# Softmax sums kept with channels on rows: a 0/1 product spreads each head's sum over its rows, VectorE divides there, and the projection follows without transposes

## What is computed

```
# self-attention
q, k, v = heads(x @ Wq + bq), heads(x @ Wk + bk), heads(x @ Wv + bv)
attn = softmax(rope(q) @ rope(k).T / sqrt(8))
out  = (attn @ v, heads side by side) @ Wp + bp
# the layer
x = x + self_attention(layernorm(x))
x = x + cross_attention(layernorm(x), ctx)     # the same form, Wo, bo
x = x + layernorm(xn + top2_experts(xn)) * gamma + beta,  xn = layernorm(x)
```

## Time and profile before

| | |
|---|---|
| median of three runs | 718.91 us (718.05 to 723.16) |
| profiled execution, its time | 726.41 us |
| profiled execution, its span | 724.6 us |
| PE busy | 586.8 us (81%) |
| DVE busy | 396.8 us (55%) |
| ACT busy | 334.2 us (46%) |
| POOL busy | 336.6 us (46%) |
| mean granted PE clock | 0.869 |
| chain that ended last: PE, DVE | 54%, 19% of the span |

### The profile page before, as it was taken

One profiled execution on the slowest core, in us unless ns is written; L12 is line 12 of the kernel. 1 busy time (PEld: TensorE's weight loads), 2 busy tenths in 40 slices (PEclk: granted clock), 3 DMA queues, 4 the chain that ended last, 5 costly groups with the idle time before them and its releaser, 6 DMA issues.

```text
span 724.6 us, 22167 instructions
## 1 busy us (share of the span) xinstructions
PE 586.8 (81%) x7694; PEld 425.6 (59%) x7695; DVE 396.8 (55%) x1325; ACT 334.2 (46%) x867; POOL 336.6 (46%) x464
## 2 busy tenths in 40 slices
PE   4638898999998898889899979841698888888791
PEld 2325665666755656656567656621597888888630
DVE  3457675767685675474563634225354444445364
ACT  2215565665755655555454633311354544445333
POOL 4415452524437446345254265355754344444365
PEclk9859999999999999898895965555799999999996
DMA  4340413140773305103112210002222211121182
GB/s 120 112 115 16 129 54 96 49 141 22 209 211 104 96 18 140 59 24 86 33 48 65 65 52 16 31 19 70 58 67 53 58 52 50 51 61 50 57 240 75
DMA packets 74424, 55.62 MB, mean 77 GB/s; under 512 B 9024, under 2 KB 70981, under 8 KB 74338
## 3 DMA queue, kind: packets, MB, share of 16 engines
q1 hardware_dynamic: 69954, 45.92, 22.5%
q0 software_dynamic: 4384, 8.53, 3.7%
HBM read 33.62 MB, written 19.23 MB: 73 GB/s over the span
## 4 chain that ended last, share of the span: by engine, by line
PE 54%; DVE 19%; issue 9%; POOL 6%; DVEq 4%; another core or an unknown queue 3%; ACT 3%; DMA 2%; SPq 1%; POOLq 0%
DVE nmp L1149 7%; PE AV L738 7%; PE AV L927 6%; PE S L915 6%; PE ST L711 5%; PE AV L831 4%; PE W L782 4%; PE SM L763 3%; DVEq L1374 3%; PE ST L717 3%; PE SM L751 2%; POOL routed L1524 2%; PE S L679 2%; DVE va L1396 2%
## 5 line engine op out<-in xcount | busy, mean ns | idle before, releaser
L1149 DVE TENSOR_REDUCE nmp<-S 128x4 bf16<-128x512 f32 (+1 forms) x256 | 142.3, 577 | 103.3 <-PE S L679 67.0
L963 ACT ACTIVATE prob<-ST 128x512 f32<-128x512 f32 (+1 forms) x256 | 138.5, 591 | 91.0 <-PE ST L717 78.8
L1083 ACT ACTIVATE va<-S,b1s 128x128 f32<-128x128 f32 x288 | 82.2, 368 | 99.3 <-PE S L915 93.1
L1586 POOL DMA_INDIRECT expert_out<-va,prob x72 | 70.9, 985 | 92.6 <-DVE va L1401 75.9
L711 PE MATMUL ST<-nmt,onesr 32*77 32x128 bf16 (+1 forms) x1024 | 82.4, 235 | 16.1 <-DVE nmp L1149 12.3
L915 PE MATMUL S<-va 128*128 128x128 f32 x576 | 81.4, 285 | 17.1 <-DVE va L1389 15.7
L738 PE MATMUL AV<-prob,va 77*32 77x128 f32 (+1 forms) x2048 | 93.9, 306 | 0.3 <-issue 0.2
L711 PEld LDWEIGHTS ST<-nmt,onesr 32*77 32x77 bf16 (+1 forms) x1024 | 59.1, 112 | 52.5 <-issue 48.5
L915 PEld LDWEIGHTS S<-va 128*128 128x128 f32 x576 | 71.3, 195 | 25.5 <-DVE va L1389 24.0
L1489 POOL TENSOR_SCALAR ve<-mv 128x1 f32<-128x1 f32 x64 | 14.8, 232 | 150.2 <-DVE mv L1183 149.9
L1524 POOL DMA_INDIRECT routed<-pay,dest x64 | 65.3, 1021 | 22.3 <-issue 16.3
(11 more groups left out here) (187 smaller groups left out, 1189.5 us busy)
## 6 DMA issues: line engine op xcount, KB each, us to landing
prob<-routed SPq DMA_DIRECT2D x72, 65.0 KB
qs<-q_parts SPq DMA_DIRECT2D x32, 128.0 KB, 3.0
ks<-k_parts SPq DMA_DIRECT2D x32, 128.0 KB
q2s<-q_parts SPq DMA_DIRECT2D x32, 128.0 KB
va<-expert_out SPq DMA_DIRECT2D x16, 256.0 KB, 4.2
k2s<-k_parts SPq DMA_DIRECT2D x32, 77.0 KB
xin<-x SPq DMA_DIRECT2D x8, 256.0 KB, 3.2
q_parts<-rpart SPq DMA_DIRECT2D x8, 256.0 KB
```

What stands on the lines that cost most here:

```text
L963: act.activation(prob[0:st.keys, j, :], ST[j % 2][0:st.keys, :], ACT.Exp, scale=SCALE).then_inc(s_exp, 1)
L1083: last = act.activation(ht[:, k, q, :], S[k][:, q * P:(q + 1) * P], ACT.Gelu, bias=b1s[:, bass.ds(b + q, 1)])
L1149: V.tensor_reduce(nmp[:, st.at % 2, row_tile(p), 0:NB], S[p % 2][:, 0:NB * st.keys].rearrange("p (b k) -> p b k", b=NB), AX.X, ALU.max, ne ...
L1586: pool.indirect_dma_start(out=expert_out, out_offset=bass.IndirectOffsetOnAxis(ap=xr[:, c % ROUND, D + 1:D + 2].bitcast(U32), axis=0), in_ ...
```

## The change

The sums stay with channels on rows. A 128 x 128 matrix of zeros and ones, `of_head`, has in row k a one in the 16 columns of a head if row k holds that head's sum. PE multiplies it with both halves of `ots` into `DEN`, so each of the 16 rows of a head gets the head's sum. DVE takes the reciprocal of the whole 128 x 256 tile and multiplies `ots` by it. The result is what the projection takes: with the weights' rows spread to the same places (`wp`, two halves), two products add up to the output, and no turn back is needed. In the padded weights the row of the first head's sum holds the bias: the sum divided by itself is 1. `wp` is made once at the start by products with a spread identity (`padded`, `first_sum`). The three-part bf16 bias (`c3`, `three_ones`) goes. `x1` has 13 rows instead of 14.

```diff
-RING = 14
+RING = 13
...
-        wself = sb("wself", [P, 2, D])
-        wcross = sb("wcross", [P, 2, D])
+        wself = sb("wself", [P, 1, D])
+        wcross = sb("wcross", [P, 1, D])
+
+        wp = sb("wp", [P, 2, 2, D])
+        of_head = sb("of_head", [P, P])
...
-        rden = sb("rden", [P, H])
-        onorm = sb("onorm", [P, H, HD])
-        onormt = sb("onormt", [P, L])
+        rden = sb("rden", [P, 2 * L])
+        onormt = sb("onormt", [P, 2 * L])
...
-        PROJ, TURNED, ROWS = SM[:, 0:D], SM[:, 0:2 * L], SM[:, 0:L]
+        PROJ, DEN = SM[:, 0:D], SM[:, 0:2 * L]
...
-            (idb[:, :], ident_bf), (wraw2, w_cross[:, 0:2, :]), (wcross[:, :, :], w_cross[:, 2:4, :]),
+            (idb[:, :], ident_bf), (wraw2, w_cross[:, 0:2, :]), (wcross[:, 0, :], w_cross[:, 2, :]), (wpraw[:, 0, :], w_self[:, 5, :]), (wpraw[:, 1, :], w_cross[:, 3, :]),
...
-            def sums_turned(st):
+            def sums(st):
+
                 pe.wait_ge(s_ot, st.at + 1)
                 if st.at:
                     pe.wait_ge(s_res, st.at)
                 for m in range(2):
-                    last = tr(TURNED[:, m * L:(m + 1) * L], ots[:, m * L:(m + 1) * L], idf[:, :])
-                last.then_inc(s_turned, 1)
-
-            def rows_turned(st):
+                    last = mm(DEN[:, m * L:(m + 1) * L], of_head[:, :], ots[:, m * L:(m + 1) * L], start=True, stop=True)
+                last.then_inc(s_den, 1)
+
+            def projected(st):
                 pe.wait_ge(s_onorm, st.at + 1)
-                tr(ROWS, onorm[:, :, :].rearrange("p h c -> p (h c)"), idf[:, :]).then_inc(s_rows, 1)
-
-            def projected(st):
-                pe.wait_ge(s_onormt, st.at + 1)
-                w = wcross[:, 1, :] if st.cross else wself[:, 1, :]
-                if st.at == 0:
-                    pe.wait_ge(s_cb, C3)
-                mm(PROJ, onormt[:, :], w, start=True, stop=False)
-                mm(PROJ, three_ones[0:96, :], c3[0:96, int(st.cross), :], start=False, stop=True).then_inc(s_proj, 1)
+                for m in range(2):
+                    last = mm(PROJ, onormt[:, m * L:(m + 1) * L], wp[:, int(st.cross), m, :], start=(m == 0), stop=(m == 1))
+                last.then_inc(s_proj, 1)
...
             pe.wait_ge(s_cb, 2)
+            pe.wait_ge(s_pad, PADS)
+            for cross in range(2):
+                for m in range(2):
+                    at = (2 * cross + m) * D
+                    last = mm(ST[1][:, at:at + D], padded[:, m, :], wpraw[:, cross, :], start=True, stop=(m == 1))
+                    if m == 0:
+                        mm(ST[1][:, at:at + D], first_sum, cfull[:, cross, :], start=False, stop=True)
+            last.then_inc(s_padded, 1)
...
                 act.wait_ge(s_av, 2 * st.at + 2)
                 if st.at:
-                    act.wait_ge(s_turned, st.at)
+                    act.wait_ge(s_onorm, st.at)
                 move(ots[:, :], SUMS, s_ot)
-
-            def rows_out(st):
-                act.wait_ge(s_rows, st.at + 1)
-                if st.at:
-                    act.wait_ge(s_proj, st.at)
-                move(onormt[:, :], ROWS, s_onormt)
...
+            act.wait_ge(s_padded, 1)
+            move(wp[:, :, :, :].rearrange("p c m d -> p (c m d)"), ST[1][:, :], s_wp)
...
-                did(V.tensor_copy(c3[:, :, :], cfull))
-                for rows in (slice(32, 64), slice(64, 96)):
-                    for quarter in range(rows.start // 32, 3):
-                        part = slice(32 * quarter, 32 * quarter + 32)
-                        did(V.tensor_tensor(cfull[part], cfull[part], c3[part, :, :], ALU.subtract))
-                        did(V.tensor_copy(c3[part, :, :], cfull[part]))
-                assert n == C3
+
+            def spread_out():
+
+                V.memset(padded, 0.0).then_inc(s_pad, 1)
+                V.memset(first_sum, 0.0).then_inc(s_pad, 1)
+                V.tensor_copy(of_head[:, :].rearrange("p (h c) -> p h c", c=VG),
+                              idf[:, HD::VG].unsqueeze(2).to_broadcast([P, P // VG, VG])).then_inc(s_pad, 1)
+                dve.wait_ge(s_pad, 3)
+                V.tensor_copy(padded.rearrange("p m (h c) -> p (m h) c", c=VG)[:, :, 0:HD],
+                              idf[:, :].rearrange("p (h c) -> p h c", c=HD)).then_inc(s_pad, 1)
+                V.tensor_copy(first_sum[:, HD:HD + 1], idf[:, HD:HD + 1]).then_inc(s_pad, 1)
...
             def norm_rows(st):
 
-                dve.wait_ge(s_turned, st.at + 1)
-                if st.at:
-                    dve.wait_ge(s_rows, st.at)
-                o = TURNED.rearrange("p (h c) -> p h c", c=VG)
-                V.reciprocal(rden[:, :], o[:, :, HD:HD + 1].rearrange("p h c -> p (h c)")).then_inc(s_rden, 1)
+                dve.wait_ge(s_den, st.at + 1)
+                V.reciprocal(rden[:, :], DEN).then_inc(s_rden, 1)
                 dve.wait_ge(s_rden, st.at + 1)
-                V.tensor_tensor(onorm[:, :, :], o[:, :, 0:HD],
-                                rden[:, :].unsqueeze(2).to_broadcast([P, H, HD]), ALU.mult).then_inc(s_onorm, 1)
+                V.tensor_tensor(onormt[:, :], ots[:, :], rden[:, :], ALU.mult).then_inc(s_onorm, 1)
...
-                G.memset(three_ones[:, :], 0.0).then_inc(s_set, 1)
-                pool.wait_ge(s_set, 5)
-                for k in range(3):
-                    G.memset(three_ones[32 * k:32 * k + 1, :], 1.0).then_inc(s_set, 1)
-                    pool.wait_ge(s_set, 6 + k)
+                pool.wait_ge(s_set, 4)
```

More of the change, by code:

```diff
@@ L274, in decoder_layer @@
         ots = sb("ots", [P, 2 * L])
-        rden = sb("rden", [P, H])
-        onorm = sb("onorm", [P, H, HD])
-        onormt = sb("onormt", [P, L])
+        rden = sb("rden", [P, 2 * L])
+        onormt = sb("onormt", [P, 2 * L])
         x2all = sb("x2all", [P, SEQS * D])
-        raw = x2all[:, 0:12 * D].rearrange("p (k d) -> p k d", d=D)
+        raw = x2all[:, 0:18 * D].rearrange("p (k d) -> p k d", d=D)
         wraw, wraw2, bprow, borow, bvb = raw[:, 0:4, :], raw[:, 4:6, :], raw[:, 6, :], raw[:, 7, :], raw[:, 8:10, :]
-        cfull = raw[:, 10:12, :]
+        cfull, wpraw, padded, first_sum = raw[:, 10:12, :], raw[:, 12:14, :], raw[:, 14:16, :], raw[:, 16, :]
         xn3all = sb("xn3all", [P, SEQS * D])
@@ L371, in decoder_layer @@
         s_nmt = sem("s_nmt")
-        s_turned = sem("s_turned")
+        s_den = sem("s_den")
+        s_pad = sem("s_pad")
+        s_padded = sem("s_padded")
+        s_wp = sem("s_wp")
         s_onorm = sem("s_onorm")
-        s_rows = sem("s_rows")
-        s_onormt = sem("s_onormt")
         s_proj = sem("s_proj")
@@ L486, in decoder_layer @@
         FIRST = (
-            (idf[:, :], ident), (wraw, w_self[:, 0:4, :]), (wself[:, :, :], w_self[:, 4:6, :]), (bself[:, :], b_self), (cosb[:, :], cos_t),
+            (idf[:, :], ident), (wraw, w_self[:, 0:4, :]), (wself[:, 0, :], w_self[:, 4, :]), (bself[:, :], b_self), (cosb[:, :], cos_t),
             (sinb[:, :], sin_t),
@@ L500, in decoder_layer @@
         )
-        SET_STEPS = 9
-        C3 = 9
+        SET_STEPS = 5
+        PADS = 5
         block = stack.enter_context(nc.Block())
@@ L851, in step @@
                 if before:
-                    sums_turned(before)
+                    sums(before)
                 background(st, 2)
                 values(st, 0)
-                if before:
-                    rows_turned(before)
                 background(st, 3)
@@ L862, in _ @@
             pe.wait_ge(s_bvb, 2)
-            mm(S[0][:, 0:D], bvb[:, 0, :], wself[:, 1, :], start=True, stop=True).then_inc(s_cbp, 1)
-            mm(S[1][:, 0:D], bvb[:, 1, :], wcross[:, 1, :], start=True, stop=True).then_inc(s_cbp, 1)
+            mm(S[0][:, 0:D], bvb[:, 0, :], wpraw[:, 0, :], start=True, stop=True).then_inc(s_cbp, 1)
+            mm(S[1][:, 0:D], bvb[:, 1, :], wpraw[:, 1, :], start=True, stop=True).then_inc(s_cbp, 1)
             pe.wait_ge(s_set, SET_STEPS)
@@ L872, in _ @@
                     maxima_turned(st)
+            pe.wait_ge(s_wp, 1)
             for st in STEPS:
@@ L876, in _ @@
             values(STEPS[-1], 1)
-            sums_turned(STEPS[-1])
-            rows_turned(STEPS[-1])
+            sums(STEPS[-1])
             projected(STEPS[-1])
@@ L1022, in step @@
             def step(st):
-                after, before, last = near(st, 1), near(st, -1), near(st, -2)
-                if last:
-                    rows_out(last)
+                after, before = near(st, 1), near(st, -1)
                 exps(st, 0)
@@ L1311, in _ @@
             bias_rows()
+            spread_out()
             dve.wait_ge(s_set, SET_STEPS)
```

12 lines of the change are left out of this document (removed).

## The result

The changed kernel took 893.13 us (median of four runs, 885.23 to 900.42); the kernel before, run beside it, 721.03 (four runs, 718.05 to 724.2). Without the 900.42 that is 1.235 times the time, with an interval from 1.223 to 1.247. The forecast was 838, with a range up to 885: the direction was right, the size was too small. The profiled execution took 895.47 us, its span is 893.6. (An execution over 1.5% above the fastest of its kernel counts as slow and is left out where kernels are compared; in experiment 3 and for the whole reciprocal in experiment 6 this leaves one time.)

What follows compares the result with a forecast made beforehand. PE's next step was taken to wait for DVE's fourth maximum, with `norm_rows` right ahead of it; 88.8 + 3 + 7 - 3 + 2 - 4 + 25 = 118.8 us gave 845 us profiled, 838 on the median, range 800 to 885.

Steps and rivals of the forecast that it cites:

- The chain: DVE's longer reciprocal and product ahead of the fourth maximum, which PE's next score products await: +1.55 us a step, +88.8 us.
- this sign: Sign expected in the changed profile: no DVE idle time between third and fourth maximum, 2.1 us apart instead of 0.5.
- the third reading: Reciprocal cost per column, taking 148 ns as fixed from a copy: 6.4 ns, giving 1.8 us for 256 columns.
- Sums product and projection: PE's longer fp32 products: sums ready 0.2 us later in about 14 cross steps, +3 us; one more projection instruction, +7 us.
- The 5.8 us of gaps: PE's waits beyond 0.15 us behind the fourth maximum in 11 of 61 steps, subtracted from the chain's 94.6 us.
- Start, end, POOL: Bias splitting gone at the start, -3 us; later last routing, +2 us; fewer waits for POOL's rows, -4 us.
- POOL's -4: Late steps where PE waits for POOL's rows: longer steps before give POOL that time, -4 us (0 to -8).
- The clock: PE's pauses in the attention steps lower its granted clock: 179 us more at the low level, 0.15 each, +25 us.
- Rival 1: PE's clock holds in the attention part, so the 25 us fall away: 813 us, or 800; chance 15%.
- Rival 2: PE's clock stays low through the whole attention part, 400 us more at the low level: 873 us; chance 18%.
- Rivals 3 and 4: Reciprocal at one column a cycle, 0.50 us: 749 us, 9%; the same with PE's clock kept high: 711 us, 2%.

Runs made afterwards that it cites:

- experiment 3: The kernel before plus an unread 256-column reciprocal between its own reciprocal and product, `x1` with 13 rows: 1.211 times the kernel before.
- experiment 6: The changed kernel with a reciprocal of 128, 192 or all 256 columns, any other divisors constant: 746.72, 813.55 and 848.51 us on one chip.
- experiment 2: The changed kernel with eight unread products on PE behind the first half of the values, in its pause: 837.5 us, 1.144 times the kernel before.
- experiment 5: The kernel before with its own small division moved behind the next step's first two maxima: 662.95 us (0.981) and 702.03 us (0.972) on two chips.

## Why the prediction was right about the direction and short in size

**The chain was right.** In all of steps 1 to 60 PE starts 0.15 us behind the fourth maximum, as forecast. In step 7 DVE is not idle in between; over these steps it is idle for 12.7 us between the third and the fourth maximum (4.1 before), mostly for the sums product, so this sign held for most steps and not for all. The reciprocal is 1.755 us (forecast 1.67, upper bound 1.8), the product 0.428 (0.42). Together +1.64 us a step instead of +1.55. The sizes from 128 to 256 columns give (1755-953)/128 = 6.27 ns a column. The forecast's slope of 5.9 from the two small sizes was 6% low; the third reading, (251-148)/16 = 6.4, was nearer. The Trainium skill, "VectorE: DVE Perf Modes", section "Walkthrough: the 8-slice pipeline in each mode", gives the reciprocal a repeat count of 8, which the prediction turned into an estimated 2.1 us; the measured 1.755 decides against eight cycles a column.

**Sums product and projection** were forecast at 3 + 7 = 10 us. In the steps at full clock the half without division grew by 0.21 us in the mean (0.16 in all but step 51): 59 x 0.21 = 12. The wait for the sums product itself was sized too small: DVE's reciprocals of steps 1 to 60 waited about 10 us, before about 2, where +3 was forecast; part of it lies in steps at the low clock. Chain, sums and projection together: forecast 98.8, measured 59 x 1.87 = 110, of which the longer reciprocal and product are 5, the gaps 5.8.

**The 5.8 us of gaps** were counted as used up by the longer chain, and the gaps did close. But the steps at full clock, from which the 1.87 comes, had none but 0.12 us in step 56, so the saving appears in the other steps, where it cannot be told from the clock's loss.

**Start, end, POOL.** DVE's first maximum of the first step came 2.0 us earlier (50.6 to 48.6), forecast 3. Behind step 60 it is +1.9, forecast +2. Of POOL's -4, one step is seen: step 58 became 2.6 us shorter, although its chain is longer.

**The clock was the step that failed, and of it the price.** The prediction expected 179 us more at the low level; the 59 steps had 191. That this came out is partly luck: it inferred the clock from PE's share of busy time, and in experiment 6 the same share, 82% of the steps' stretch, went with 0.90 at 128 columns and with 0.78 at 192. It found 0.25 to 0.33 us for each in the earlier trace rows (the pair behind the 0.33 is not quite alike, with 13 and 9 instructions on DVE) and halved this: "In a changed step about half (maxima, reciprocal and product, some 3.4 of 8 us) runs at DVE's pace whatever PE's clock, so I take half, 0.15." That assumes that the low stretches fall evenly on both halves. They don't. In step 7 the half with the division has clock 1.00 and the half behind the pause 0.65; summed over 61 steps (1 to 61), 226 of 291 us at the low level lie in the halves that PE sets. In the kernel before it was 71 of 91, the same 78%, so its trace could have told. In step 7 the 3.4 low microseconds cost some 1.5, a price of 0.4, since PE was the bound in all of them. On average it was 0.30, the price of the earlier trace rows without the halving. With it the prediction's own sum would have been 88.8 + 10 - 5 + 179 x 0.30 = 147.5, and 866 us on the median. The whole error, 169.0 against 118.8 us, divides so: 32 for the clock (57 against 25; 29 of it the halved price, the rest the 12 us more at the low level), 11 for chain, sums and projection (110 against 98.8), and 6.5 for start, end and POOL (+1.5 outside the steps against -5; what POOL gave back lies in the steps). That is 50 us over the forecast for the profiled execution (845).

**The rivals.** Rival 1 (the clock holds) fell in the changed kernel, and is what experiment 2 looks like. Rival 2 gave 873, nearest to the result, but by another way: a clock at the low level throughout. It was not: the mean in the steps is 0.75, and twelve steps ran at 1.00. Its nearness is luck. Rivals 3 and 4, a cheap reciprocal, fell with the first group read. The page "TensorE: Matmul & The Clock Gate" of the Trainium skill, section "HAM oscillation — how this bites in real kernels", tells of bursts that start cold behind every wait. The trace agrees with it in kind (of 276 us at the low level 256 lie outside PE's pauses, in its products, and filling the pause brought the clock from 0.74 to 0.91), not in the strict form that rival 2 stood for: half of the steps' time was at the high level, and twelve steps wholly.

## What to carry to other kernels

Read the order on the engine that others wait for before its load: the same 112 us of reciprocals made the kernel 170 us slower in front of the fourth maximum than in the gap behind the second, and in the gap the large division with the change's PE products cost 21 to 36 us, not nothing. Compare kernels with the same order before calling work free. When an engine is made to pause, look where the low clock lands afterwards; if it lands in the products that bound the step, a price read off such steps (0.30 us for each at the low level here) is not to be halved. Ask the same of an instruction that is there already: moving the old half-microsecond division out of that place gave 2 to 3%.

## What the runs showed of the hardware that was not expected

- A reciprocal of fp32 on 128 rows takes 180 ns for 4 columns, 253 for 16, 953 for 128, 1355 for 192, 1755 for 256: 6.27 ns a column, against 1.04 for a product.
- PE's clock loss did not grow in proportion to the reciprocal: over the kernel before, the time at the low level was 19 us more with 128 columns, 143 with 192 and 174 with 256, in kernels equal but for that.
- Chips differ by 6 to 8% for the same kernel (676 and 721 to 731 us), a part of it in the expert stage: 147 to 148 against 160 to 167 us from its first to its last activation. The attention steps do not all differ: experiment 5's kernel took 69.2 and 78.0 us for steps 1 to 12 and 13 to 26 on both chips, at clock 1.00. Steps 27 to 40 then took 78.7 us at 1.00 on one and 90.7 at 0.92 on the other, and steps 41 to 52 58.6 and 67.7, both at 1.00. Why was not found.
